# A graph attention kernel: six gathers in flight instead of four, and each step's rows stored in two parts

## The reference

```
h = layernorm(x) @ W                      # 6250 x 256, four heads of 64
e = leaky_relu(a_src[src] + a_dst[dst])   # one logit per edge and head
alpha = softmax of e over the edges of one destination
x = x + relu(segment_sum(alpha * h[src], dst) + bias)
```

```
h = h + 0.01 * tanh(h);  h = h * sigmoid(h);  h = layernorm(h) @ W.T + b
```

## Time and profile before

| | |
|---|---|
| median of three runs | 4365.51 us |
| profiled execution, its own time | 4401.49 us |
| its span | 4399.7 us |
| `prepare` | 0 to 276.5 us |
| `attend` | 276.5 to 2609 us |
| `scan_ffn` | 2609 to 4399.7 us |
| busy over the span | PE 39%, DVE 67%, ACT 37%, POOL 73% |
| moved by all transfers | 491.41 MB, 112 GB/s over the span |

### The profile page before, as it was taken

How to read it: one execution, slowest core, us unless ns; L and a number is a source line. 1 busy time by engine, 2 the same in 40 slices (tenths; PEclk the granted TensorE clock), 3 DMA queues, 4 the chain that set the end, 5 groups by cost and what they waited for, 6 DMA issues and landing times. The chain is left out here.

```text
span 4399.7 us, 55666 instructions
## 1 busy us (share of the span) xinstructions
PE 1722.1 (39%) x9318; PEld 1498.1 (34%) x9318; DVE 2942.3 (67%) x9723; ACT 1607.2 (37%) x3892; POOL 3198.9 (73%) x3325
## 2 busy tenths in 40 slices
PE   2410000000000000000000000999999999999997
PEld 1200000000000000000000000888888888888886
DVE  6345555555555555555555556888888888888887
ACT  1201101011111111101011117777777777777775
POOL 3556666666666666666666647999999999999996
PEclk9655555555555555555555555999999999999998
DMA  6235555555555555555555542000000000000001
GB/s 190 71 115 175 186 191 191 190 191 191 192 190 192 191 189 186 182 190 192 190 192 190 191 160 91 1 0 0 0 0 0 0 0 0 0 0 0 0 0 58
DMA packets 127434, 491.41 MB, mean 112 GB/s; under 512 B 50089, under 2 KB 51370, under 8 KB 111332
## 3 DMA queue, kind: packets, MB, share of 16 engines
q0 software_dynamic: 84624, 235.32, 18.1%
q1 hardware_dynamic: 41188, 254.16, 16.3%
q10 hardware_dynamic: 1536, 1.18, 0.2%
HBM read 254.95 MB, written 236.40 MB: 112 GB/s over the span
## 5 line engine op out<-in xcount | busy, mean ns | idle before, releaser
L727 POOL DMA_INDIRECT G<-haug,idx x1612 | 1527.5, 948 | 806.8 <-issue 481.9
L1259 PE MATMUL ps_g<-WT,h2T 128*128 128x256 f32 x6000 | 1420.6, 380 | 0.0
L1259 PEld LDWEIGHTS ps_g<-WT,h2T 128*128 128x128 f32 x6000 | 1082.9, 190 | 116.5
L1001 POOL TENSOR_TENSOR h<-Hs,th 128x512 f32<-128x512 f32 x750 | 956.4, 1275 | 16.5 <-ACT th L1070 9.8
L1235 PE MATMUL ps_x<-tdiag,ones 128*128 128x512 f32 x2 | 2.1, 1141 | 2353.2 <-DVE tdiag L1086 2353.2
L1193 DVE SCALAR_TENSOR_TENSOR Hs<-ps_g,r,b 128x256 f32 (+1 forms) x1500 | 700.5, 467 | 226.7 <-PE ps_g L1259 212.1
L1235 PEld LDWEIGHTS ps_x<-tdiag,ones 128*128 128x128 f32 x2 | 0.5, 310 | 2353.5 <-DVE tdiag L1086 2353.5
L833 DVE SCALAR_TENSOR_TENSOR G<-G,keep,ps_m 128x260 f32<-128x260 f32 x1488 | 705.2, 474 | 45.9 <-remote 14.2
L746 ACT ACTIVATE lz<-bm 128x4 f32<-128x4 f32 x124 | 26.0, 210 | 1816.9 <-issue 1055.3
L783 DVE TENSOR_TENSOR z<-G,AD 128x52 f32<-128x52 f32 x124 | 30.3, 245 | 954.3 <-DMA G<-haug,idx 954.0
L818 DVE TENSOR_TENSOR ps_m<-G,ps_w 128x260 f32<-128x260 f32 x1612 | 648.8, 423 | 0.4 <-issue 0.4
(11 more groups left out here) (149 smaller groups left out, 1018.2 us busy)
## 6 DMA issues: line engine op xcount, KB each, us to landing
sums<-G SPq DMA_DIRECT2D x124, 1716.0 KB
G<-haug,idx POOLq DMA_INDIRECT x1612
haug<-hrow SPq DMA_DIRECT2D x7, 924.0 KB
own<-haug SPq DMA_DIRECT2D x7, 924.0 KB, 4.7
X<-x SPq DMA_DIRECT2D x7, 784.0 KB, 24.5
out<-X SPq DMA_DIRECT2D x7, 784.0 KB
adz<-raw SPq DMA_DIRECT2D x4, 830.5 KB, 35.2
raw<-adz SPq DMA_DIRECT2D x1, 3224.0 KB, 10.3
```

The costliest lines, as they stand in the source:

```text
L727: pool.indirect_dma_start(out=G[:, u, t, :], out_offset=None, in_=haug[:, :], in_offset=bass.IndirectOffsetOnAxis(ap=idx[:, u, t:t + 1], a ...
L1001: g.tensor_tensor(h1[:, u, :], chunk_rows(Hs, j0 + u), th[:, u, :], ALU.add).then_inc(s_add, 1)
L1259: last = nc.tensor.matmul(ps_g[u][:, a * C:(a + 1) * C], h2T[:, u, (a * 2 + k) * P:(a * 2 + k + 1) * P], WT[:, k, :], start=(k == 0), stop ...
```

## The change

The constant `FLY` goes from 4 to 6, so six semaphores take turns and gather n waits for gather n - 6. A new constant `HALF` is 6. The store of a step becomes two: `store_head` stores rows 0 to 5 (811,008 bytes) and waits for the step's maxima in `G` (`s_max`) and for the add of row 5 (`s_half`, new); `store_tail` stores rows 6 to 12 (946,176 bytes) under the condition that the one store had. Both raise `s_st[u]`, so POOL waits for 32 per turn instead of 16. On DVE add 5 now raises `s_half` instead of the chain's semaphore, and add 6 waits for `s_half` and for its own message.

```diff
-FLY = 4
+FLY = 6
+HALF = 6
...
-                def store(i, u):
+                def store_rows(k, u, t0, t1):
+                    sp.dma_start(sums[0:EPAD, :].rearrange("(p c) f -> p c f", c=CW)[:, bass.ds(k * T + t0, t1 - t0), :],
+                                 G[:, u, t0:t1, :]).then_inc(s_st[u], 16)
+
+                def store_head(i, u):
 
                     k = i * R + u
-                    if isinstance(k, int) and k == STEPS - 1:
-                        sp.wait_ge(s_max, STEPS)
+                    sp.wait_ge(s_max, k + 1)
+                    sp.wait_ge(s_half, k + 1)
+                    sp.nop(nofuse=True)
+                    store_rows(k, u, 0, HALF)
+
+                def store_tail(i, u):
+
+                    k = i * R + u
+                    if k == STEPS - 1:
                         sp.wait_ge(s_sums, STEPS)
                     else:
                         sp.wait_ge(s_carried, k + 2)
                     sp.nop(nofuse=True)
-                    sp.dma_start(sums[0:EPAD, :].rearrange("(p c) f -> p c f", c=CW)[:, bass.ds(k * T, T), :],
-                                 G[:, u, :, :]).then_inc(s_st[u], 16)
+                    store_rows(k, u, HALF, T)
...
-                    stages = [(load_idx, 0), (store, R)]
+                    stages = [(load_idx, 0), (store_head, R), (store_tail, R)]
...
-                    sp.wait_ge(s_st[u], TURNS * 16)
+                    sp.wait_ge(s_st[u], TURNS * 32)
...
-                        wait_count(pool, s_st[u], i * 16)
+                        wait_count(pool, s_st[u], i * 32)
...
-                            ch.wait(max(at["m", t], at["s", t - 1]))
+                            if t == HALF:
+                                dve.wait_ge(s_half, k + 1)
+                                ch.wait(at["m", t])
+                            else:
+                                ch.wait(max(at["m", t], at["s", t - 1]))
...
+                        elif t == HALF - 1:
+                            ins.then_inc(s_half, 1)
```

More of the change, by code:

```diff
@@ L675, in attend @@
         s_carried = sem("s_carried")
+        s_half = sem("s_half")
         s_sums = sem("s_sums")
```

## The result

The changed kernel takes 4097.91 us (median of four runs, 4097.71 to 4099.53) against 4363.36 (4359.72 to 4368.48) in the same comparison: a ratio of 0.9392, 95% interval 0.9375 to 0.9408, faster by 265 us. On a second chip it was 4098.51 against 4375.18, ratio 0.9368 (0.9351 to 0.9385). The prediction was 4088 in a range of 4065 to 4160. The profiled execution took 4097.84 us with a span of 4096.0, where 4124 had been forecast for it; this one is not above the median of its runs, as the one of before was by 36 us.

A forecast was written before the change was run, and what follows sets the result against it. Bound in `attend` by POOL's gathers stalling behind each step's store, 287 us in all. Saved 272.8 + 2.3 + 2.3 = 277.4 us, so 4365.5 - 277.4 = 4088 us, range 4065 to 4160.

The forecast's parts named there:

- Rival D: In `attend`, the stall comes once per 13 gathers from their own queue, not the store; no change, 4366 us; chance 0.03.
- B: The gathers' queue in `attend` takes no more than four, so only the split works: 4165 us; chance 0.05.
- A: In `attend`, part of the stall stays, half a stall per step, 136 us lost: 4224 us; chance 0.07.
- by 0.27 us only: Six gathers in flight allow 7.52 us, enough even behind a whole store, where a gather lands in 7.25.
- two us of spare: With the split, a gather lands after 5.54 us behind the tail, 5.15 behind the head, against 7.52 allowed.
- the shorter last store: After the last gather, the last store holds the next block; its tail is shorter by 2.3 us.
- The price of a part: Each store part holds the transfer engines for its bytes only: head 2.28 us, tail 2.67.
- The fair turns: Transfer engines alternating fairly between queues by packet would delay a gather about 1.8 us, without stall; the 7.0% contradicts it.
- What hides the waits: DVE's three added waits per step, at most 0.9 us, lie beside its 5.6 us idle; taken as nothing.
- The wait at step 6: Early in `attend`, step 6 starts at 388.73 after step 2's store lands; said to remain, tail landing 2.3 us earlier.
- the 36 us: The kernel before's profiled execution exceeded its runs' median by this; none in the stalls gives 4088, all gives 4124.
- The pitch: POOL's unstalled time per gather in `attend`, 1.254 us, 16.30 per step; expected to be the next limit.

The follow-up runs named there:

- the doubled store: Kernel before with six in flight and the whole store issued twice, the second time to a scratch tensor: 4369.88 us against 4102.93 with one store.
- the second trace of before: The kernel before, unchanged, profiled once more: 4371.76 us in the profiled execution, runs of the same kernel on that chip at 4375.18.
- the run with small pieces: Kernel before with rows of `G` 32 bytes apart, so the store goes in pieces of 1056 bytes instead of 13,728: 4372.85 us, ratio 1.0025.

## Why the prediction was right

*The cause.* That one store per step holds the gathers past the time that four in flight allow is shown from both sides: by five in flight (1.25 us more allowed, 0.92 of stall per step left of 2.2), by six (0.03 left), and by the store divided and spread (0.30 left). Rival D, a stall of the gathers' own queue, falls with the last of these and with the doubled store, which change nothing but the store and move the stall. B falls because six in flight with the whole store is as fast as 4103 us, with the gather's instruction unchanged at 946 ns. A falls with no stall at all in the changed kernel. What makes the gathers wait inside the transfer engines is not shown, only for how long and beside what.

*Six in flight would do alone, "by 0.27 us only".* It nearly does, with 4 us of stall in 124 steps. But the 0.27 us were no margin: the 7.25 us was read from one step, and in the run with six and the whole store the longest gather takes 7.5 us to land and 36 gathers still wait for one (8.2 us is the longest in the second trace of before). That six was just enough for a whole store is in part luck. The split on top was to give two us of spare and no time of its own but the shorter last store. It gave 5 us: those 4 of stall, and 1.8 for the last store, from the last gather to the next block 25.3 us in the second trace of before, 23.5 in the changed kernel (2281.18, then 2304.73):

```profile
2281.18 0.95 POOL L739 DMA_INDIRECT G<-haug,idx  x1 [0.30 <-issue]
...
2304.73 0.80 SPq L965 DMA_DIRECT2D own<-haug  x2
```

*The price of a part.* I took its bytes, 2.28 and 2.67 us. The engine time of the store's queue did not rise: 28.1% of 1600 us over 99 steps is 4.5 us per step (4.5 to 4.7 in the five traces with the parts apart), against 4.95 (4.8 to 4.9 in three more traces with one store). The landings have a part that doesn't go with the bytes: 6.7 us for 1716 KB against 4.5 for 924 KB are 2.2 us for 792 KB, which leaves 1.9 us for no bytes, an estimate; the head's 4.3 us for 792 KB give 2.2. The Trainium skill (DMA: Bandwidth & Descriptors, Anatomy of one DMA) puts a fixed 2.0 us on a transfer that GpSimd issues; these are SP's, and their landings lie near it. But this is time to the landing, not time in which the engines are held, and so it cost nothing here.

*The fair turns.* The prediction took one packet of the profile, 0.60 us, for one turn, and found that the 7.0% don't fit. That is not quite what the page says: in the Trainium skill (the same page, Queues, rings and completion order) a packet is a group of descriptors, 9 to 17 as a rule and 64 at most, that an engine drains before it switches. The store has 128 pieces of 13,728 bytes for 16 engines, 8 for each. If such a piece is one descriptor, that is less than one packet of the page, and the rule would let a whole store go ahead of a gather. So the earlier trace rows rule out turns of one piece, and the run with small pieces (104 for each engine, the stall unchanged) does so again; whether the turns are as long as the page allows, or not fair, no run here tells.

*What hides the waits.* DVE from `z` to its last message takes as long as before and waits for 5.7 us per step (705.9 / 124), as forecast (5.6); the three added waits are lost in that.

*The size.* 277 us were forecast off the median and 265 came in one comparison, 277 in the other, where the kernel before was 12 us slower and the changed one the same. Two terms were off, in opposite directions. The wait at step 6, which was to remain because it "hangs on DVE", was no part of the kernel: it is absent from the second trace of before and from the changed kernel. With the other stalls ahead of step 6 the sum left 14 of the 287 us in place (287 less 272.8), and they went too. And the stalls, read as 287 us, are 271 in that second trace; the first was a long execution. That 14 left in and 16 read too many nearly cancel is luck; so is it that 4088 was chosen as if none of the 36 us lay in the stalls, where the second trace puts more than half of the excess there. The pitch, read as 1.254 us from the first step, is 1.250 over the stage (2281.18 - 267.32 us over 1611), 6 us in all. The 30 iterations stayed within 0.3 us, `prepare` did not gain from the deeper flight: the first gather starts at 266.7 to 268.8 us in four more traces of kernels with four in flight, and at 266.9 to 268.1 in those with six.

## What to carry to other kernels

A limit on transfers in flight is an allowance in time: the number times the pitch of issue. Compare it with the longest time to land, beside the largest other transfer, and not with the usual one; here 2.9 us alone became 7.3 beside a store in the step read, and up to 8.2 in a whole trace. Once the allowance covers it, a higher number or smaller stores bring next to nothing (here 5 us of 4098), so of two remedies take the cheaper one, here the constant alone.

## What the runs showed that was not expected

The changed kernel's time hardly varies between occasions and chips (4097.9 and 4098.5) while the kernel before varies (4362 to 4375 in the medians, and 4362 and 4370 on one and the same chip). No gather waits in the changed kernel, so it seems to be free of what the transfers do; what varies in the kernel before is not shown. In the steps read here the gathers get 5 to 7% of the engines beside a large transfer from SP's queue, whatever its pieces, but about three times that beside a second one queued behind it (5.8% and 16.8%). And 0.305 us pass between two gather instructions whether or not a wait stands between them; with the 0.945 of the instruction that makes 1.25 x 1612 = 2015 of the 2037.7 us of `attend`.
